# An eight-stage network on one core: softplus computed in PSUM, one scan per tile, wide GpSimd products, and a new list order

## The reference, cut to what matters

```python
xc = silu(dwconv(xs)); zc = silu(dwconv(zs)); u = xc
dt, Bm, Cm = split(u @ x_proj_w)
delta = softplus(dt @ dt_proj_w + dt_proj_b)
dA = exp(delta * A); dBu = delta * Bm * u
h[t] = dA[t] * h[t-1] + dBu[t]           # per sequence, 16 states for each of 128 channels
y[t] = sum over states of h[t] * Cm[t]  + u * Dp
x = x + out_proj(concat(y, zc))
x = x + mlp(ln(x)) , mlp with a bias b2 at its end
```

## Time and profile before

| | |
|---|---|
| median of 3 runs (lowest to highest) | 1385.8 us (1383.31 to 1387.94) |
| the profiled execution's own time | 1385.3 us |
| its span, first to last instruction | 1383.5 us |
| mean granted clock of TensorE | 0.968 |
| busy: PE, DVE, ACT, POOL | 1280.2, 941.4, 896.0, 789.7 us |
| chain that ended last, by engine | PE 65%, DVE 11%, POOL 9%, ACT 8%, issue 5%, DMA 2% |
| transfers | 67.86 MB, 49 GB/s |

### The profile page before, as it was taken

The page is one execution under the profiler, slowest core; times in us unless marked ns, Lnnn a source line. Parts: engine busy times, 40 slices in busy tenths (PEclk is TensorE's granted clock), DMA queues, the critical chain, the costliest instruction groups (busy, mean ns, idle before and its releaser), DMA issues.

```text
span 1383.5 us, 26286 instructions
## 1 busy us (share of the span) xinstructions
PE 1280.2 (93%) x8734; PEld 909.6 (66%) x8734; DVE 941.4 (68%) x3661; ACT 896.0 (65%) x2495; POOL 789.7 (57%) x876
## 2 busy tenths in 40 slices
PE   8577988899977889999999999999999999999997
PEld 4233655567644666677767867777777867886665
DVE  5989868677568677757563663485988659864253
ACT  6736689787474679767787676556568664775231
POOL 2998666576378556466556756355435325450534
PEclk9868899899998999999999999999999999999999
DMA  8742000101141100110010001301020030001431
GB/s 285 193 122 76 9 9 2 55 2 55 55 103 28 37 1 1 55 65 1 1 63 1 1 1 63 125 1 62 2 81 1 1 93 1 2 2 70 115 91 32
DMA packets 23109, 67.86 MB, mean 49 GB/s; under 512 B 2336, under 2 KB 9120, under 8 KB 20672
## 3 DMA queue, kind: packets, MB, share of 16 engines
q1 hardware_dynamic: 22976, 66.20, 15.2%
HBM read 62.85 MB, written 3.34 MB: 48 GB/s over the span
## 4 chain that ended last, share of the span: by engine, by line
PE 65%; DVE 11%; POOL 9%; ACT 8%; issue 5%; DMA 2%; SPq 0%; POOLq 0%; DVEq 0%; ACTq 0%
PE bank L1064 57%; PE bank L1068 8%; ACT arena L1514 6%; POOL arena L2315 3%; DMA arena<-cf 2%; DVE arena L1769 2%; DVE arena L2261 2%; POOL arena L2386 1%; DVE arena L2254 1%; DVE arena L2012 1%; POOL arena L2385 1%; POOL arena L2328 1%; DVE arena L1947 1%; DVE arena L2010 1%; DVE stats L1783 1%
## 5 line engine op out<-in xcount | busy, mean ns | idle before, releaser
L1514 ACT ACTIVATE arena<-arena 128x256 f32<-128x256 f32 (+4 forms) x808 | 357.9, 447 | 64.7 <-DVE arena L2012 32.5
L1514 ACT ACTIVATE arena<-bank 128x512 f32<-128x512 f32 (+3 forms) x355 | 190.7, 563 | 230.3 <-PE bank L1064 144.5
L1064 PE MATMUL bank<-XT,W 128*128 128x512 f32 (+1 forms) x752 | 290.2, 523 | 1.0 <-DVE arena L1775 0.6
L1064 PEld LDWEIGHTS bank<-W,arena 128*128 128x128 f32 x1888 | 231.5, 193 | 52.5 <-issue 39.4
L1064 PE MATMUL bank<-W,arena 128*128 128x128 f32 (+1 forms) x1888 | 243.4, 279 | 6.2 <-POOL arena L2328 3.1
L2385 POOL TENSOR_TENSOR arena<-arena 128x256 f32<-128x256 f32 x192 | 117.6, 613 | 220.8 <-DVE arena L2018 220.0
L1064 PE MATMUL bank<-arena 128*32 128x128 f32 (+8 forms) x2912 | 228.0, 336 | 16.2 <-ACT arena L1514 7.4
L2328 POOL TENSOR_TENSOR arena<-arena 128x512 f32<-128x512 f32 (+1 forms) x108 | 170.8, 1601 | 93.7 <-DVE arena L1769 39.0
L1064 PEld LDWEIGHTS bank<-arena 128*32 128x32 f32 (+4 forms) x2912 | 154.8, 153 | 81.1 <-issue 45.2
L1068 PE MATMUL bank<-CF,arena 128*128 128x128 f32 x1312 | 182.1, 279 | 23.9 <-POOL arena L2386 10.7
L2386 POOL TENSOR_TENSOR arena<-arena 128x512 f32<-128x512 f32 x192 | 199.7, 1040 | 0.0
(11 more groups left out here) (138 smaller groups left out, 1700.5 us busy)
## 6 DMA issues: line engine op xcount, KB each, us to landing
arena<-rws SPq DMA_DIRECT2D x8, 2048.0 KB, 7.4
arena<-rep SPq DMA_DIRECT2D x62, 256.0 KB, 5.9
arena<-rws SPq DMA_DIRECT2D x4, 1792.0 KB, 6.6
W<-w SPq DMA_DIRECT2D x2, 2124.0 KB, 8.6
arena<-rws SPq DMA_DIRECT2D x8, 384.0 KB, 10.4
W<-w SPq DMA_DIRECT2D x1, 2692.0 KB, 9.3
XT<-wkq SPq DMA_DIRECT2D x4, 512.0 KB, 8.3
W<-w SPq DMA_DIRECT2D x1, 2005.0 KB, 15.5
```

What stands on the lines that cost most here:

```text
L1064: return e.matmul(o, lhsT, rhs, start=start, stop=stop, skip_group_check=True)
L1514: return e.activation(o, a, func, **kw)
```

## The change

Nine things are changed:

1. Softplus works in the PSUM bank of `0.dt`: exp, `0.dr` and the sum of `0.du` write there. A new ACT step `0.dc` copies delta to SBUF, and `0.da` waits for it in place of `0.du`. The bank is held until `0.dc`.
2. The first token of each sequence gets delta 0 and no exponential, so that its decay is 0, and one scan runs over all 512 tokens.
3. `0.db` covers two tiles (128x1024) at once, and needs both landings.
4. C stays in its PSUM bank from `0.bc` to the last `0.ac`, and the products `0.hc` on DVE read it there; POOL's read the copy.
5. `0.b` and `0.x` are gone. PE adds b2 by four matmuls with one row in `0.o`, and DVE doubles the residual in `0.y`.
6. The columns of stage 0's weights are laid out anew, and stage 4's weights are loaded over those of the convolution: the load waits for the last `0.in` and `0.dt` of all chunks, not for `0.e`.
7. `1.km` may go to either engine.
8. The tables `PARTS`, `AHEAD`, `URGENT`, `HASTE`, `STAY` have other numbers, and `HASTE` may name a chunk or a stage.
9. The lists of all engines come out in another order.

```diff
+    "0.dt": "P.87 A2.35 V.67", "0.ln": "A.63", "0.dr": "V2.10", "0.du": "V1.42", "0.dc": "A.59", "0.f": "P.25 A.28", "0.st": "V1.17", "0.hc": "V.69|G1.28", "0.db": "G2.36", "0.ac": "P.88",
+    "0.y": "V.68 P1.80 V1.28", "0.m": "V1.68 G1.25 A1.62 P.45 A.74", "0.h": "P.87 A.69", "0.o": "P4.45 V.70",
...
-HELD = {("0.ac", 0): [("Y", 0, ("0.y", 0, 0), 4, 1)],
+HELD = {("0.dt", 0): [("b", 0, ("0.dc", 0, 0), 1, 1)], ("0.bc", 0): [("c", 0, ("0.ac", 3, 0), 1, 1)], ("0.ac", 0): [("Y", 0, ("0.y", 0, 0), 4, 1)],
...
-                add("0.da", q, ("0.du", 0), ("0.a", 0, PREP), *([("0.st", q - 3)] if q >= 4 else []))
-            if by == "0.rp":
-                add("0.db", q, (by, q), ("0.bc", 0))
+                add("0.da", q, ("0.dc", 0), ("0.a", 0, PREP), *([("0.st", q - 3)] if q >= 4 else []))
+            if by == "0.rp" and q % 2:
+                add("0.db", q // 2, (by, q - 1), (by, q), ("0.bc", 0))
...
-STAY = {"stay": 5809.00, "act": 0.61}
+STAY = {"stay": 26906.00, "act": 0.08}
...
+                key = (t - HASTE.get(x.name, 0.0) - HASTE.get((x.name, x.c), 0.0) - HASTE.get((x.s, x.c), 0.0) + other, -x.tail - AHEAD.get((x.s, x.c), 0.0)
...
+                elif name == "0.dc":
+                    act(later(step0(c, 0)), later(bank[b.i][:, :]), ACT.Copy).then_inc(done[b.i], 1)
...
-                    act(bank[a.i][:, :], bank[a.i][:, :], ACT.Exp, scale=am[:, g:g + 1], bias=am[:, 16 + g:17 + g])
+                    act(later(bank[a.i][:, :]), later(bank[a.i][:, :]), ACT.Exp, scale=am[:, g:g + 1], bias=am[:, 16 + g:17 + g])
...
+                    own(stt(ps[:, :], s0(c, 14), 1.0, ps[:, :], ALU.subtract, ALU.subtract))
+                    own(stt(ps[:, :], s0(c, 4), 1.0, ps[:, :], ALU.add, ALU.mult))
+                    own(stt(ps[:, :], ps[:, :], -0.5, s0(c, 11), ALU.mult, ALU.add))
...
+                    own(e.memset(step0(c, 0).rearrange("p (b l) -> p b l", b=2)[:, :, 0:1], 0.0))
+                    own(tt(ps[:, :], ps[:, :], s0(c, 12), ALU.add))
+                    tt(step0(c, 1), ps[:, :], s0(c, 6), ALU.mult).then_inc(has["du"], 1)
...
-                    own(e.tensor_tensor_scan(h[:, 0:256], bank[a.i][:, 0:256], h[:, 0:256], 0.0, ALU.mult, ALU.add))
-                    e.tensor_tensor_scan(h[:, 256:512], bank[a.i][:, 256:512], h[:, 256:512], 0.0, ALU.mult, ALU.add
-                                         ).then_inc(done[a.i], 1)
+                    e.tensor_tensor_scan(h, bank[a.i][:, :], h, 0.0, ALU.mult, ALU.add).then_inc(done[a.i], 1)
...
-                    tt(ring0(c, n), ring0(c, n), s0(c, 16), ALU.mult).then_inc(has["hc_v"], 1)
+                    tt(ring0(c, n), ring0(c, n), bank[cc.i][:, :], ALU.mult).then_inc(has["hc_v"], 1)
...
+                    stt(rows(0, c), rows(0, c), 2.0, bank[b.i][:, :], ALU.mult, ALU.add).then_inc(done[b.i], 1)
...
+                    if s == 0:
+                        for j in range(4):
+                            mm(ps[:, j * 128:(j + 1) * 128], cst("one", 1), wt(0, "b2", 0, 1), j == 0, False)
...
-                    e.tensor_tensor(h, h, s0(c, 8), ALU.mult).then_inc(has["dB"], 1)
+                    e.tensor_tensor(h, h, s0(c, 8).unsqueeze(1).to_broadcast([128, 2, 512]), ALU.mult).then_inc(has["dB"], 1)
```

More of the change, by code:

```diff
@@ L46 @@
 FIRST = 148
-FIRST0 = 1816
+LATE0 = 1924
 CONSTB = [("mask", 384)]
@@ L267, in stage_steps @@
             add("0.h", j, ("0.m", 0))
-        add("0.x", 0, ("0.m", 0), ("0.b", 0, PREP))
-        add("0.o", 0, ("0.x", 0), *[("0.h", j) for j in range(4)])
+        add("0.o", 0, *[("0.h", j) for j in range(4)])
         add("0.e", 0, ("0.o", 0))
@@ L349, in weight_steps @@
 def weight_steps():
-    loads = [("load", s, 0, [("f" if q else "0.e", 0, c, q) for q in OVER[s] for c in range(NC)]
+    loads = [("load", s, 0, [need for q in OVER[s] for c in range(NC) for need in ([("f", 0, c, q)] if q else [("0.in", 1, c, 0), ("0.dt", 0, c, 0)])]
               + [("4.st", n, PREP, 0) for n in range(4) if s == 4]) for s in OVER]
@@ L1159, in _ @@
                                  ring0(c, 4 * n + j), n == 0, n == 3)
+                        if n == 3 and j == 0:
+                            ins.then_inc(done[uses["c", "0.bc", c, 0].i], 1)
                     ins.then_inc(full[b.i], 1)
@@ L1592, in _ @@
                 elif name == "0.bc":
-                    for k, to in (("b", s0(c, 8)), ("c", s0(c, 16))):
-                        b = u(k, name, c)
-                        evict(b, to, bank[b.i][:, :])
+                    b, cc = u("b", name, c), uses["c", name, c, 0]
+                    evict(b, s0(c, 8), bank[b.i][:, :])
+                    on.wait_ge(*filled(cc))
+                    act(s0(c, 16), bank[cc.i][:, :], ACT.Copy).then_inc(has["c"], 1)
                 elif name == "0.f":
@@ L1602, in _ @@
                     act(s0(c, 12), bank[b.i][:, :], ACT.Abs, bias=wt(0, "dtb")).then_inc(has["sf_a"], 1)
-                    act(s0(c, 11), bank[b.i][:, :], ACT.Relu, bias=wt(0, "dtb")).then_inc(done[b.i], 1)
+                    act(s0(c, 11), bank[b.i][:, :], ACT.Relu, bias=wt(0, "dtb")).then_inc(has["sf_r"], 1)
                     on.wait_ge(*after("sf_a", name, c))
-                    act(s0(c, 13), s0(c, 12), ACT.Exp, scale=-1.0).then_inc(has["sf_e"], 1)
+                    on.wait_ge(*after("sf_r", name, c))
+                    act(bank[b.i][:, :], s0(c, 12), ACT.Exp, scale=-1.0).then_inc(has["sf_e"], 1)
                     act(s0(c, 4), s0(c, 12), ACT.Tanh, scale=0.5).then_inc(has["sf_t"], 1)
+                elif name == "0.dc":
+                    b = u("b", "0.dt", c)
+                    on.wait_ge(*after("du", "0.du", c))
+                    act(later(step0(c, 0)), later(bank[b.i][:, :]), ACT.Copy).then_inc(done[b.i], 1)
                 elif name == "0.ln":
@@ L1615, in _ @@
                     on.wait_ge(*filled(a))
-                    act(bank[a.i][:, :], bank[a.i][:, :], ACT.Exp, scale=am[:, g:g + 1], bias=am[:, 16 + g:17 + g]).then_inc(has["dA"], 1)
+                    act(later(bank[a.i][:, :]), later(bank[a.i][:, :]), ACT.Exp, scale=am[:, g:g + 1], bias=am[:, 16 + g:17 + g]).then_inc(has["dA"], 1)
                 elif name == "0.h":
@@ L1961, in _ @@
                     on.wait_ge(*filled(b))
-                    tt(s0(c, 2), bank[b.i][:, :], rows(0, c), ALU.add).then_inc(done[b.i], 1)
+                    own(tt(s0(c, 2), bank[b.i][:, :], rows(0, c), ALU.add))
+                    stt(rows(0, c), rows(0, c), 2.0, bank[b.i][:, :], ALU.mult, ALU.add).then_inc(done[b.i], 1)
                 elif name == "0.m":
@@ L1967, in _ @@
                     b = u("b", name, c)
-                    on.wait_ge(*after("x0", "0.x", c))
+                    on.wait_ge(*emptied(u("b", "0.y", c)))
                     on.wait_ge(*filled(b))
-                    tt(s0(c, 2), bank[b.i][:, :], s0(c, 2), ALU.add).then_inc(done[b.i], 1)
+                    tt(s0(c, 2), bank[b.i][:, :], rows(0, c), ALU.add).then_inc(done[b.i], 1)
                 elif name == "1.m" and p == 1:
@@ L1989, in _ @@
                     on.wait_ge(*after("kq", "1.kq", c, 0))
-                    for i in (0, 2):
+                    for i in (n, n + 2):
                         ins = ts(km1(c)[:, i * 512:(i + 1) * 512], s1(c, 3), cst("hm")[:, i:i + 1], None, ALU.mult)
```

151 lines of the change are left out of this document (82 added, 69 removed), and 244 rows, old and new, of tables (AHEAD, EMITS, HASTE, OPENS).

## The result

| kernel | median us | runs | ratio to before, 95% interval |
|---|---|---|---|
| before | 1386.48 (1383.31 to 1387.94) | 4 | |
| changed | 1367.22 (1361.93 to 1369.96) | 4 | 0.986 [0.9825, 0.9894] |

The forecast was 1370, within 1343 to 1394. The profiled execution took 1369.96, with a span of 1368.0; the sum had 1368. Its clock was 0.961. The fastest of the four runs had 0.974. The changed kernel varies more from run to run (8.0 us) than the one before (4.6).

The account below looks back on a forecast made before the run. PE bounds the kernel, except in the first chunks' scans, where DVE and POOL are nearly full. Four stretches, 147 + 267 + 40 + 914, give a span of 1368; with 1.8 and 0.5 added, 1370 us, range 1343 to 1394.

Parts of the forecast that it names:

- forecast case: Whole kernel: 1370 us from a span of 1368, reaching from 1358 to 1380 by its uncertain terms; chance 0.48.
- Stretch one: To the third chunk's last `0.ac`, POOL and DVE nearly full: 18 us shorter, its mark from 165 to 147.
- Who blocks whom: POOL's `0.db` products: about half blocked for some 0.5 us, held to be by DVE's products of two SBUF tensors.
- The softplus: DVE, second and third chunk: six operations go from 1.592 to 0.685 us each, 5.4 us less.
- The wide products: POOL, before the third chunk's last `0.ac`: 23 at 2.365 us replace 46 `0.db` at 1.535, 16.2 us less.
- no change: Rival, 1385 us, chance 0.14: POOL's wide products stay blocked at 3.07 (16 us), or ACT's table loads cost 14 us.
- The single scan: DVE: one scan of 512 in place of two of 256 saves 0.05 us a tile, 2.4 us for 48 tiles (0 to 8).
- Stretch two: To chunk 3's first decays: 216 us of PE work at 0.81 for each us take 267, mark at 414.
- denser: Rival, 1350 us, chance 0.22: the first chunk's attention fills PE while the third scans; stretch two takes 243, 24 less.
- Stretch three: Chunk 3's scans, to its last `0.ac`: POOL's 34 us of work at 87% make 40; ends 34 and 57.
- Stretch four: From chunk 3's last `0.ac` to the end: 852 us of PE work at the old factor 1.073 take 914.
- Slower: Rival, 1397 us, chance 0.16: held banks make scans wait for decays, 27 us; decides from 3.3 us a group.

Follow-up runs that it names:

- all four undone: The changed kernel with C and the softplus in SBUF, two narrow products on POOL and two scans, in its own new lists: 1383.17 us, 0.9976.
- control: The changed kernel timed once more, with no edit, for the other runs to be read against: 1362.34 us, 0.9841.
- the fourth experiment: The changed kernel with each wide product of stage 0 on POOL as two narrow ones of 512, C and softplus in PSUM: 1360.4 us, 0.9819.

## Why the prediction was right, step by step

The forecast case came: 1370 against 1367.2, faster by more than 0.3%. What it rested on, that the time per operation falls on DVE and POOL and with it the first stretch, was confirmed. That the sum of 1368 is the measured span to the microsecond is luck: its four terms are off by +5, +3, +5 and -13, and the next execution profiled had 1360.3. The gain in ratios times 1386, read along one chain from before to the changed kernel:

| step | ratios | us |
|---|---|---|
| lists, earlier load, no `0.x`, small edits | 1 to 0.9976 | -3.3 |
| one scan | 0.9976 to 0.9952 | -3.3 |
| C and softplus in PSUM | 0.9952 to 0.9819 | -18.4 |
| wide products | 0.9819 to 0.9841 | +3.0, inside the intervals |

The lengths of the four stretches (us, from the marks of the profiled executions) say where each step acts:

| kernel | one, from 0 | two | three | four |
|---|---|---|---|---|
| before | 164.3 | 226.9 | 56.5 | 935.8 |
| all four undone | 165.8 | 265.2 | 44.9 | 901.8 |
| C and softplus in SBUF, narrow products, one scan | 165.1 | 265.2 | 44.9 | 901.6 |
| narrow products | 148.2 | 265.2 | 43.4 | 901.1 |
| changed (control) | 150.7 | 265.3 | 43.6 | 900.7 |

The operands act almost alone in stretch one, as forecast: 16.9 of the 18.8 us between the third and the fourth row. Stretches two to four have their lengths by the lists, the load and the small edits, nearly whatever these operations cost.

**Stretch one** was forecast to shorten by 18, to 147. It ended at 152.1, and at 150.7 in the control. The busy times were right (DVE about 105 forecast, 102.6 measured; POOL 100.8 and 101.4). The step that failed is "both engines get 18 to 20 us shorter, and I take 18 for the stretch": the stretch shortens with the busy time only where the idle time stays. DVE's rose from 11.3 to 21.4, and POOL's from 18.6 to 22.6. The edits that shortened DVE left it waiting for ACT's decays (10.8) and PE's matmuls (10.2), hardly for POOL (0.8), and POOL waiting for DVE's scans (14.3).

**Who blocks whom** was the weakest ground of the forecast ("I don't see what blocks a product"). The runs show it: with DVE's two SBUF inputs gone, all 39 `0.hc` of POOL take 1.26 to 1.28; with them back, POOL pays about 0.45 at a time, and a DVE product of 0.68 takes up to 2.84. That PSUM is simply the quicker place for an operand is ruled out by the products of 0.68 with both inputs in SBUF. The Trainium skill (SBUF — State Buffer, "Who interferes with whom") says that whichever of the two comes first holds the shared ports for its whole instruction, and that a DVE instruction with one SBUF input stays out of it. This case agrees: 0.677 with C in PSUM, 1.43 with C in SBUF beside narrow products, 1.52 beside wide ones; POOL's delay of 0.45 is less than the 0.68 of such a product, though. The same section lets a scalar operation with its fast mode compete too, which fits `1.km` at 1.37 and 2.49.

**The softplus** was priced at 5.4 us for its six operations, beside narrow products. There they measure 1.459 against 0.697, 4.6, so the term was right in size; left out were the two sums of `0.du`, 1.65 against 0.70, another 1.9. Beside the change's wide products moving it back cost 13.0: the six went from 0.70 to 2.18, 8.9, and the two sums to 2.73, 4.1. And it is a chain ahead of each chunk's scans, not filling among them.

**The wide products** were booked as POOL's largest saving, 16.2. As the fourth experiment shows, 12.0 of it belong to the PSUM operands (9.4 when both are measured in the same lists). The sum was right and its owner wrong. The *no change* case spoke of wide products at 3.07; they came at 2.36, yet its time is about what the change would have had without the PSUM operands (1390.05), with wide products at 2.59 and most of the loss on DVE.

**The single scan**, 2.4 (0 to 8): 3.3 and 4.9 measured, neither clear of the intervals.

**Stretch two**, 216 us of work at 0.81: it took 269.9, a rate of 0.80. The *denser* case did not come (its own sum, 24 less than 1370, would be 1346 and not 1350); ACT, which spoke against it, was busy 206.7 of 270, with 21 table loads in it.

**Stretch three**, 40: it took 45.0, and 43.6 in the control, within its bounds. The step that failed is the ground for it, POOL's cheaper products at the same 87% of the stretch. POOL was busy 33.6 of the 45.0, as counted, but that is 75%; and with all four parts undone the stretch takes 44.9 too. It is shorter than the 56.5 of before because of the lists. The clock was at 0.70 there (0.88 before), so PE's emptier list made its own matmuls slower. For that the forecast had one us, 39 made 40.

**Stretch four**, 914: it took 901.0, 13 less, and made up for the other three. The step that failed is the factor 1.073, taken over from the stretch before. Of the old idle time of 27.2 us only 17.8 are left, and "what that is worth is inside the rate" set the earlier load at nothing. Late, with the lists that follow, it costs 26 to 28. That is more than the whole gain, while lists and load together are worth 3.3. I take it that the new lists are built on the early load and lose elsewhere most of what it gives, which no run shows by itself.

***Slower*, by banks**: it did not come. DVE's idle time before scans rose from 5.0 to 7.8 (10.8 in one execution), but the banks held are not what raised it: in the four runs with C in SBUF the same banks are held, and it is 5.4 to 5.7. As I read it, it rises when DVE's other work gets shorter and DVE comes to its scans earlier. It stays below the 3.3 us for each group that the case needed; the largest such wait in the control is 2.36. Waiting bank by bank changed nothing.

**What stays open**: whether narrow products are really better. Both runs with them lie at 1360 to 1362 at the median, and the nine of the changed kernel at 1359 to 1370; the intervals overlap. The run with narrow products, 0.9819, is the fastest version measured and beats the kernel before. Also open is the single scan, and what each of the small edits inside the first 3.3 us is worth. C and the softplus were undone together beside narrow products, so their shares are known beside wide ones only (14.8 and 13.0).

## What to carry to other kernels

When two engines both look full, ask whether part of their busy time is each waiting for the other: a form whose duration has two prices in the trace is the sign, and moving one operand to PSUM can be worth much: here 18.4 us, against 3.3 for new lists and an earlier load together. Look at the shortest, the median and the longest of such a form, and at what runs beside each. Price such an edit on both engines, and put work that heads a chain at its full length, not among the engine's filling. And do not carry a stretch's factor over to a new order when a load in front of it has moved: its idle time is the first thing that changes.

## What the hardware showed that was not expected

- The exchange between DVE and POOL is lopsided. A DVE product of two SBUF tensors takes 0.68 where POOL runs nothing, the same as with one PSUM input, and up to 1.76 beside narrow and 2.84 beside wide products; the means are 1.43 and 1.52. At the mean, a softplus operation went from 0.70 to 1.46 and 2.18. POOL's products rose by 0.2 at the mean (1.27 to 1.48) or 0.13 to 0.23 (2.36 to 2.49 and 2.59). A wider POOL instruction, which spares POOL 0.19 us a pair, can cost 10.5 us in all when DVE shares its operands' memory.
- One program gave 1358.6 to 1370.0 us with mean clocks from 0.975 to 0.961. Two profiled executions differ in how long PE ran at the low level in two gaps; that this makes the whole of the spread is not shown, and the clock alone doesn't order the runs (0.972 gave 1358.6, 0.975 gave 1361.9).
